# A state scan beside a feed-forward network: the sum over states one step earlier, background operations two or three steps later

## The reference

```python
x = layernorm(x + L0_attn(x))                                   # attention phase of the kernel
x = layernorm(x + (silu(x @ W1.T) * (x @ W3.T)) @ H @ W2.T)     # first network
# state scan, 32 states for each of the 512 features, 4 sequences of 512 tokens
delta = softplus(dt + b_dt)
h = exp(delta_t * A) * h + (delta_t * u_t) * B_t                # one step in t
y_t = einsum('bdn,bn->bd', h, C_t)
x = layernorm(x + y + u * D_param)
x = layernorm(x + (silu(gate) * up) @ w_down.T)                 # second network
```

## Time and profile before

| | us |
|---|---|
| median of 3 runs | 2284.1 |
| lowest and highest | 2273.91 and 2285.38 |
| the profiled execution | 2278.88 |
| its span | 2277.1 |
| TensorE busy in it | 2058.8 |
| VectorE, ScalarE, GpSimd busy | 1482.9, 956.8, 1333.1 |

### The profile page before, as it was taken

One profiled execution on the slowest core, in us unless ns is written; L12 is line 12 of the kernel. 1 busy time (PEld: TensorE's weight loads), 2 busy tenths in 40 slices (PEclk: granted clock), 3 DMA queues, 4 the chain that ended last, 5 costly groups with the idle time before them and its releaser, 6 DMA issues. The chain is left out here.

```text
span 2277.1 us, 27746 instructions
## 1 busy us (share of the span) xinstructions
PE 2058.8 (90%) x9456; PEld 1272.9 (56%) x9456; DVE 1482.9 (65%) x1794; ACT 956.8 (42%) x1597; POOL 1333.1 (59%) x1015
## 2 busy tenths in 40 slices
PE   8899999589998899888989889998899999999997
PEld 6767676357854444444444445444455555456785
DVE  2525325244337878687877889877889999995333
ACT  4333231343245445544556454445445544443212
POOL 4222311245317977688877898656887798683210
PEclk9899999799999999998999999999999999999999
DMA  5000100346634455455545554323434334333552
GB/s 192 20 19 19 37 18 9 130 157 239 247 137 141 170 178 179 144 163 183 157 163 179 188 174 148 110 83 98 148 125 139 107 123 137 120 135 129 184 184 77
DMA packets 100607, 301.20 MB, mean 132 GB/s; under 512 B 25792, under 2 KB 38592, under 8 KB 83712
## 3 DMA queue, kind: packets, MB, share of 16 engines
q1 hardware_dynamic: 100480, 299.62, 38.9%
HBM read 228.28 MB, written 71.30 MB: 132 GB/s over the span
## 5 line engine op out<-in xcount | busy, mean ns | idle before, releaser
L1461 POOL TENSOR_TENSOR h_times_c<-h_states,c_rep 128x512 f32<-128x512 f32 x512 | 667.4, 1319 | 285.5 <-PE scan_y L1100 265.1
L1233 ACT ACTIVATE delta_spread<-delta_spread,a_neg 128x512 f32<-128x512 f32 x512 | 338.7, 662 | 336.8 <-PE delta_spread L1072 335.9
L1345 DVE TENSOR_TENSOR d_b<-du_spread,b_rep 128x512 f32<-128x512 f32 x384 | 263.6, 687 | 90.9 <-PE du_spread L1091 83.9
L1423 POOL TENSOR_TENSOR h_lo<-silu_in_h_lo,h_hi 128x512 fp32r<-128x512 f32 x128 | 171.3, 1338 | 255.1 <-ACT h_hi L1159 255.1
L1315 DVE TENSOR_TENSOR x<-x,y_or_aux 128x512 f32<-128x512 f32 x256 | 171.8, 671 | 182.2 <-PE y_or_aux L80 182.2
L78 PE MATMUL gate<-x_hi,w 128*128 128x512 f32 x512 | 278.2, 543 | 7.4 <-POOL x_lo L1428 5.2
L78 PE MATMUL y_or_aux<-h_hi,w 128*128 128x512 f32 x512 | 263.4, 514 | 21.2 <-ACT b_rep L1201 12.2
L1365 DVE TENSOR_TENSOR_SCAN h_states<-delta_spread,d_b 128x512 f32<-128x512 f32 x192 | 233.6, 1217 | 66.1 <-ACT delta_spread L1233 61.0
L78 PE MATMUL up<-x_hi,w 128*128 128x512 f32 x512 | 270.0, 527 | 0.0
L1365 DVE TENSOR_TENSOR_SCAN h_states<-delta_spread,h_last,d_b 128x512 f32<-128x512 f32 x192 | 244.7, 1277 | 33.3 <-ACT delta_spread L1233 33.1
L1072 PE MATMUL delta_spread<-stack,selectors 96*128 96x512 bf16 x512 | 202.6, 396 | 68.3 <-DVE h_states L1365 67.6
(11 more groups left out here) (158 smaller groups left out, 3710.9 us busy)
## 6 DMA issues: line engine op xcount, KB each, us to landing
w<-w_split SPq DMA_DIRECT2D x112, 1024.0 KB, 4.8
w<-w_split SPq DMA_DIRECT2D x112, 512.0 KB, 5.7
w_split<-w_presplit SPq DMA_DIRECT2D x48, 512.0 KB, 3.9
w_split<-w SPq DMA_DIRECT2D x16, 1024.0 KB, 6.3
spread_parts<-squares_or_parts SPq DMA_DIRECT2D x16, 768.0 KB, 4.0
stack<-spread_parts SPq DMA_DIRECT2D x96, 128.0 KB, 5.3
h_times_c<-in_w13a SPq DMA_DIRECT2D x16, 512.0 KB, 4.3
w_split<-w SPq DMA_DIRECT2D x16, 512.0 KB, 6.5
```

Source lines behind the costliest of these rows:

```text
L1233: act.activation(dl[:, s % ND], dl[:, s % ND], ACT.Exp, scale=a[:, column(s):column(s) + 1]).then_inc(s_da, 1)
L1345: dve.tensor_tensor(db[:, by_dve(s) % NB], uu[:, i % NU], brep[:, tile_of(s // SPO) % 2], ALU.mult).then_inc(s_db, 1)
L1423: pool.tensor_tensor(hl[:, idx % 4], sg[:, idx % 4], hh[:, idx % 4].bitcast(F32), ALU.subtract).then_inc(s_hl, 1)
L1461: pool.tensor_tensor(hc[:, s % NC_], hs[:, s % NH], crep[:, tile_of(s // SPO) % 2], ALU.mult).then_inc(s_hc, 1)
```

## The change

The same instructions in another order. `LAG` goes from 6 to 5, so the sum of quad q stands in scan step 4q + 8. Parts: `part_high` in P + 2 and P + 3, `part_rest` in P + 3 and P + 4, `part_mid` in P + 5 and P + 6, `part_low` in P + 6 and P + 7, the store in P + 8; `step_size` and `step_input` stay at P and P + 1. Presplit weights: high cast T + 4, rest T + 5, store T + 6, and in SyncE's step the store now stands ahead of a load; the load stays at T. Norms of width 1: squares from b + 3 instead of b + 2, variance in b + 9 instead of b + 6, scaling behind it; width 2 is as before. The tables for what follows a norm move by two to six steps. The load of the next stack stands in step 18 of 32 instead of 14.

```diff
@@ -652,17 +652,17 @@
...
-NORM_TICK = (-11, 4, 16, 28, 109, 205, 274, 301, 403, 415, 493, 532, 589, 658, 685, 781)
+NORM_TICK = (-11, 4, 16, 28, 109, 205, 277, 301, 403, 418, 493, 532, 589, 658, 685, 781)
...
-PARTS_TICK = ((121, 139, 147, 155), (236, 244, 252, 260), (332, 340, 348, 356), (445, 452, 459, 466))
...
+PARTS_TICK = ((121, 139, 147, 155), (239, 247, 255, 263), (335, 343, 351, 359), (449, 455, 461, 467))
...
@@ -679,14 +679,15 @@
     return [start + k // width for k in range(KD)]
+SQUARE_DELAY, VAR_DELAY = {1: 3, 2: 1}, {1: 9, 2: 3}
...
-VAR_AT = {b + 3 * (3 - w): e for e, (b, w) in enumerate(zip(NORM_TICK, NORM_WIDE))}
+VAR_AT = {b + VAR_DELAY[w]: e for e, (b, w) in enumerate(zip(NORM_TICK, NORM_WIDE))}
 CENTRE_AT, SQUARE_AT, SCALE_AT = {}, {}, {}
 for e_, (b_, w_) in enumerate(zip(NORM_TICK, NORM_WIDE)):
     for k_ in range(KD):
         CENTRE_AT.setdefault(stretch(b_ + 1, w_)[k_], []).append((e_, k_))
-        SQUARE_AT.setdefault(stretch(b_ + 3 - w_, w_)[k_], []).append((e_, k_))
-        SCALE_AT.setdefault(stretch(b_ + 3 * (3 - w_) + 1, w_)[k_], []).append((e_, k_))
+        SQUARE_AT.setdefault(stretch(b_ + SQUARE_DELAY[w_], w_)[k_], []).append((e_, k_))
+        SCALE_AT.setdefault(stretch(b_ + VAR_DELAY[w_] + 1, w_)[k_], []).append((e_, k_))
...
@@ -696,7 +697,7 @@
 PRE_AT = at_tick(PRE_TICK)
-SCALE_TICK_END = {e: b + 3 * (3 - w) + 1 + (KD - 1) // w for e, (b, w) in enumerate(zip(NORM_TICK, NORM_WIDE))}
+SCALE_TICK_END = {e: b + VAR_DELAY[w] + 1 + (KD - 1) // w for e, (b, w) in enumerate(zip(NORM_TICK, NORM_WIDE))}
 PARTS_BEFORE_NORM = [sum(tick < b for row in PARTS_TICK for tick in row) for b in NORM_TICK]
...
@@ -765,7 +766,7 @@
     w13x = nc.dram_tensor("w13_split", (2, NC, P, 2, 2, KD * P), F32, kind="Internal").ap()
     w2x = nc.dram_tensor("w2_split", (2, NC, P, 2, D), F32, kind="Internal").ap()
     parts_d = nc.dram_tensor("spread_parts", (NO, P, 2, 3, TT), BF16, kind="Internal").ap()
-    ND, NU, NB, NH, NC_, LAG = 2, 2, 2, 6, 7, 6
+    ND, NU, NB, NH, NC_, LAG = 2, 2, 2, 6, 7, 5
     W13, W2 = 3, 4
     with ExitStack() as ctx:
         p = Prog(nc, ctx)
@@ -946,16 +947,16 @@
                         w13_load((tick + 13) // 6)
                     if pos < HC and NC <= HC * unit + pos < CHUNKS:
                         w2_load(HC * unit + pos)
+                    if tick - 6 in PRE_AT:
+                        pre_store(PRE_AT[tick - 6])
                     if tick in PRE_AT:
                         pre_load(PRE_AT[tick])
-                    if tick - 4 in PRE_AT:
-                        pre_store(PRE_AT[tick - 4])
-                    if tick - 6 in PARTS_AT:
-                        parts_store(*PARTS_AT[tick - 6])
-                        if PARTS_AT[tick - 6] in ((0, 0), (0, 1)):
-                            stack_load(PARTS_AT[tick - 6][1])
+                    if tick - 8 in PARTS_AT:
+                        parts_store(*PARTS_AT[tick - 8])
+                        if PARTS_AT[tick - 8] in ((0, 0), (0, 1)):
+                            stack_load(PARTS_AT[tick - 8][1])
                     o, step = divmod(tick - SCAN_TICK, SPO)
-                    if step == 14 and 2 <= o + 1 < NO:
+                    if step == 18 and 2 <= o + 1 < NO:
                         stack_load(o + 1)
                     for e in NORM_AT_END:
                         if tick == SCALE_TICK_END[e]:
@@ -1285,16 +1286,16 @@
                         w2_high((tick - 1) // 6)
                     if tick in SOFT_AT:
                         soft(*SOFT_AT[tick])
-                    if tick - 1 in PARTS_AT:
-                        part_high(*PARTS_AT[tick - 1], 0)
                     if tick - 2 in PARTS_AT:
-                        part_high(*PARTS_AT[tick - 2], 1)
+                        part_high(*PARTS_AT[tick - 2], 0)
                     if tick - 3 in PARTS_AT:
-                        part_mid(*PARTS_AT[tick - 3], 0)
-                    if tick - 4 in PARTS_AT:
-                        part_mid(*PARTS_AT[tick - 4], 1)
-                    if tick - 2 in PRE_AT:
-                        pre_high(PRE_AT[tick - 2])
+                        part_high(*PARTS_AT[tick - 3], 1)
+                    if tick - 5 in PARTS_AT:
+                        part_mid(*PARTS_AT[tick - 5], 0)
+                    if tick - 6 in PARTS_AT:
+                        part_mid(*PARTS_AT[tick - 6], 1)
+                    if tick - 4 in PRE_AT:
+                        pre_high(PRE_AT[tick - 4])
             @block.vector
             def _(dve):
@@ -1482,16 +1483,16 @@
                         w13_low((tick + 10) // 6)
                     if (tick - 2) % 6 == 0 and 0 <= (tick - 2) // 6 < NC:
                         w2_low((tick - 2) // 6)
-                    if tick - 2 in PARTS_AT:
-                        part_rest(*PARTS_AT[tick - 2], 0)
                     if tick - 3 in PARTS_AT:
-                        part_rest(*PARTS_AT[tick - 3], 1)
+                        part_rest(*PARTS_AT[tick - 3], 0)
                     if tick - 4 in PARTS_AT:
-                        part_low(*PARTS_AT[tick - 4], 0)
-                    if tick - 5 in PARTS_AT:
-                        part_low(*PARTS_AT[tick - 5], 1)
-                    if tick - 3 in PRE_AT:
-                        pre_low(PRE_AT[tick - 3])
+                        part_rest(*PARTS_AT[tick - 4], 1)
+                    if tick - 6 in PARTS_AT:
+                        part_low(*PARTS_AT[tick - 6], 0)
+                    if tick - 7 in PARTS_AT:
+                        part_low(*PARTS_AT[tick - 7], 1)
+                    if tick - 5 in PRE_AT:
+                        pre_low(PRE_AT[tick - 5])
```

More of the change, by code:

```diff
@@ L659 @@
 NORM_AT_END = (10, 12, 14, 15)
-SPLIT_TICK = (-6, 11, 166, 270, 366, 474, 544, 664)
-RANK_TICK = (115, 217, 313, 427)
-DT_TICK = ((118, 127, 130, 133), (220, 223, 226, 229), (316, 319, 322, 325), (430, 433, 436, 439))
-STATES_TICK = ((121, 124), (232, 235), (328, 331), (442, 445))
-SOFT_TICK = (((119, (0,)), (135, (1, 2, 3))), ((231, (0, 1, 2, 3)),), ((327, (0, 1, 2, 3)),), ((441, (0, 1, 2, 3)),))
-PARTS_TICK = ((121, 139, 147, 155), (236, 244, 252, 260), (332, 340, 348, 356), (445, 452, 459, 466))
+SPLIT_TICK = (-6, 11, 167, 275, 370, 475, 547, 664)
+RANK_TICK = (115, 220, 316, 433)
+DT_TICK = ((118, 127, 130, 133), (223, 226, 229, 232), (319, 322, 325, 328), (436, 439, 442, 445))
+STATES_TICK = ((121, 124), (235, 238), (331, 334), (448, 451))
+SOFT_TICK = (((119, (0,)), (135, (1, 2, 3))), ((234, (0, 1, 2, 3)),), ((330, (0, 1, 2, 3)),), ((447, (0, 1, 2, 3)),))
+PARTS_TICK = ((121, 139, 147, 155), (239, 247, 255, 263), (335, 343, 351, 359), (449, 455, 461, 467))
 PRE_BLOCKS = 3 * NC
```

## The result

The changed kernel took 2304.9 us (median of 4 runs, 2298.4 to 2308.4) beside 2279.8 for the kernel before in the same comparison: ratio 1.0107, 95% interval 1.0068 to 1.0146. It is slower by 25 us where 52 us of gain were forecast, and lies outside the range. The profiled execution took 2308.4 us, span 2306.6.

What follows compares the result with a forecast made beforehand. Bound: waits among engines in the scan, 127.8 us TensorE idle plus at most 41 us of low clock. Stretch gains of 60 us, less 6 (presplit) and 2 (start), gave 52: 2278.9 to 2227 us, range 2195 to 2250.

Steps and rivals of the forecast that it cites:

- part 4: Presplit weights: SyncE reaches the store later, in about a third of 48 blocks behind a 1 MB load; net cost 6 us.
- parts 1 to 3: Earlier sum, later parts steps and later norms in the scan: shorter waits, together 60 us of gain summed by stretch.
- the third rival: Presplit store lands behind weight loads: 16 blocks, 4 us of ScalarE waiting each, half felt: 32 us, 2253; chance 0.09.
- the fifth stretch: Scan from 1246 to 1371 us, with parts work: loss 24 us, cap 12 by GpSimd's load, forecast gain 9.
- part 5: Start of the scan: first part's casts, lows and store two steps later; cost 2 us, bounds 0 and 3.7.
- The second and third stretch: Scan from 769 to 955 us, store's waits, gain 6; and 955 to 1070 us, parts work, gain 18.
- The last: The rest of the scan, after 1665 us: loss 13 us, mostly norm work that stays; forecast gain 3.
- Part 1: LAG 6 to 5: GpSimd one step, 1.86 us at least, closer to TensorE; most d_b product waits within reach.
- Parts 2 and 3: Parts: waits of 4.47 or 2.3 us shrink under 1 or go; norms: centring waits near 1.3 us should go.
- Part 6: Stack loads four steps later still have eight steps, at least 15 us, before the first spread reading them: cost nothing.
- GpSimd as the bound: First rival: GpSimd, 91% busy from 1246 to 1371 us, stays late; parts stretches give 12 instead of 38: 2253; chance 0.13.
- the second rival: VectorE starved by GpSimd: ten of 16 step sizes 5.1 us longer, +51 against some 26 of gain: 2304; chance 0.10.

Runs made afterwards that it cites:

- e5: The kernel before with only the presplit weights' cast, rest and store two steps later, as in the changed kernel: 2311.6 us, ratio 1.0160.
- e3: The changed kernel with the presplit weights' cast, rest and store, and SyncE's order, put back to the old steps: 2250.6 us, ratio 0.9873.
- e4: e3 with LAG back at 6, so only the parts and norms are as in the changed kernel: 2266.9 us, ratio 0.9941.
- e1: The kernel before with LAG 5 alone: 2283.1 us, ratio 1.0034.
- e10: e3 with `leave` one step earlier, in step 6 of an output block instead of 7: 2247.3 us, ratio 0.9859.
- e12: e10 with squares and variances of the width 1 norms back at their old distances: 2251.2 us, ratio 0.9868.

## Why the prediction was wrong, point by point

**The step that failed is part 4, the presplit weights**: "I take a net cost of 6 us and keep 0 to 32 for the range." It measured 36 us alone (e5, 28 to 45 by the interval) and 53 in the changed kernel (e3), above the upper bound. Of the 77 us between the forecast gain of 52 and the measured loss of 25, 47 are this part; some 28 are parts 1 to 3. The place was named rightly (SyncE stands at the next load and reaches the store behind a weight load) and so was the third rival; its size was wrong in three terms.

The first is the count. The prediction has a load of 1 MB before the store in about a third of the 48 blocks. By the written order that is right, 14 blocks; but it leaves out the 512 KB loads, of which 14 more stand there. Together they are 28 loads, in 22 blocks, two in 6 of them, whatever the engines do. The second is the delay. The prediction gave ScalarE about 4 us in 16 blocks, 64 us; the store landed 3.6 us later behind one load and 4.5 behind two (7.9 and 8.8 us after the rest instead of 4.3), so the price of a block was near right, but there were 22 of them. Most of it is the store's own way, 6.9 and 7.5 us from issue to landing instead of 3.9; its issue comes only 0.5 and 1 us later. The third is the share that reaches TensorE. The prediction took half of ScalarE's waiting; from e3 to the kernel after the wait grew by 60 us (43.1 to 102.8) and the time by 53, nearly all of it, and from the kernel before to e5 the wait grew by 53 and the time by 36, two thirds. The scan's exponentials stand behind the waiting cast, and the clock fell too (0.89 in the fifth stretch; 0.92 at the same steps in e3).

**Parts 1 to 3** were to give 60 us in all and gave some 32: e3 is 29 below the kernel before, with some 3 us for the start (part 5) already paid. By stretches e3 against before reads:

```profile
776.50:949.40 172.90, 163.82 (x705) 87.42 (x704) 147.56 (x174) 90.38 (x178) 149.63 (x118) 0.99 0.55 185
949.40:1046.20 96.80, 84.93 (x357) 45.08 (x356) 83.74 (x93) 53.83 (x100) 85.96 (x69) 0.93 0.55 188
...
1218.40:1348.20 129.80, 109.95 (x453) 58.68 (x452) 109.84 (x118) 66.30 (x108) 111.46 (x89) 0.92 0.53 179
...
1536.10:1633.00 96.90, 87.16 (x367) 46.38 (x366) 80.48 (x96) 55.48 (x103) 85.00 (x68) 0.95 0.40 139
1633.00:2040.60 407.60, 383.55 (x1703) 210.37 (x1702) 371.83 (x431) 184.36 (x314) 312.08 (x244) 1.00 0.36 122
```

The same steps took 186, 117, 125, 104 and 396 us before. The second and third stretch gave 13 and 20, more than the 6 and 18 forecast; the seventh 7 of 11. The fifth was to give 9 and lost 5: VectorE is busy 8 us longer there with the same instructions (101.8 to 109.8), while GpSimd, named as the cap, is 86% busy (91% before). The last, outside the presplit and the parts, was to give 3 and lost 12, and that goes with LAG: at the same steps it takes 396 and 399 us with LAG 6 (e5, e4) and 405 and 408 with LAG 5 (e1, e3), and TensorE stands idle for 24 us there in e3 instead of 12. GpSimd's waits for VectorE's scan in this stretch rise from 2.8 us in one wait to 33.6 in 38. No run shows why the closer order loses here what it gains elsewhere.

**Part 1** had two errors. "I cost this wait at nothing" held for the products: no wait of TensorE for them is among its larger ones, and the shortest gap from product to sum is 3.5 us where 2.2 were forecast. But the sum has a second condition that I did not price: the first sum of a block overwrites the PSUM bank that `leave` reads, and `leave` did not move. That is the new wait of 15.4 us in 8; its removal in e10 brought 3 us. The larger error is in what a GpSimd close behind VectorE does to VectorE. The prediction reasoned that such a GpSimd "runs out of ready work sooner". It does (its waits for VectorE's scan go from 19.8 us in 9 to 125.4 in 100 in e1), and yet it lengthens VectorE's two-operand instructions more (53 to 82 us of stretching in e1).

**Parts 2 and 3** held in mechanism: the wait for the rest of the parts went from 32.3 to 3.7 us, that for centring from 48.1 to 19.8. Together they gave 13 us (e4); the norms' share is 2 to 4 (e12), which can't be told from none.

**Part 5** forecast 2 us with bounds 0 and 3.7. From the first rank matmul to the first decay spread 40.4 us passed before, 43.9 in e4, 44.0 in e3 and 45.8 after. But it is 42.4 in e1 and 42.2 in e5, which keep the parts' old distances; so these cost between 1.6 and 3.6, and the forecast may well be right. It showed ahead of the store, not behind it (store to first spread 9.4 us, 9.7 before), so the sign that I gave for it pointed at the wrong place. **Part 6** held: TensorE's only wait for a stack load is the one at the start, 2.7 us (1.2 before).

**The rivals.** The third held, at nearly twice its price (26 us above the forecast's 6, measured 47 above). The second gave 2304 us, and the kernel took 2304.9, by coincidence: its mechanism is worth some 64 us in e10, which is 32 us faster than the kernel before, and most of the stretching (53 of 78 us) was there before the change. GpSimd as the bound is not shown: in the fifth stretch, where a gain stayed out, it is 86% busy in e3.

**The signs that were named** for part 4 told the truth: a wait of 100 us and more was to mean the third rival, and it is 102.8. GpSimd's wait for the sum did turn into waits for VectorE's scan (106.7). The d_b product's wait was to fall under a third and fell to under a half; the third stretch was to fall under 15 us of idle time and has 18.9 (104.5 less 85.6). The step sizes gave a mixed sign: their median stayed at 1.35 us, under 2, but the longest took 7.72, over the 6.5 that was to speak for the second rival. The sign for being wrong, idle time that stays, came true in the scan (140.1 us), though with other waits in front.

What stays open: how much of the 53 us is the lower clock and how much the waits themselves. The lower level lasted 148 us in e3 and 205 in the kernel after, so it can hold 28 us at most; no run holds the clock fixed. Nor was it tried to give the store a queue of its own.

## What to carry to other kernels

When a step is moved later on an engine that issues DMAs in order, look at what it is moved behind, not only at how far: every transfer that stands between in the written order goes first, and the one you moved lands behind all of them. Count all of them, small ones too, from the order before you run; here that count, 28, could be read from the step tables. Putting the store back behind its load was worth 47 us here, and moving the whole chain, load included, cost nothing that could be measured. And an order that brings GpSimd closer behind VectorE has to be weighed against VectorE's instructions with two operands from SBUF: the same edit, LAG 5, cost 8 us or gave 16 or 21, depending on what stood beside it.

## What the runs showed of the hardware that was not expected

A VectorE instruction with two operands from SBUF does not get in between GpSimd instructions that follow one another without a gap: a 128x512 one of 0.69 us took 7.72 us while six of GpSimd's, 1.3 us each, went through. The same engine reducing one operand of the same size took 659 to 686 ns in all 16 cases, 14 of them beside a GpSimd instruction; the same operation with one of its two operands in PSUM took 658 to 693 ns in all 384 cases, 318 of them beside a GpSimd instruction. The Trainium skill says in "SBUF — State Buffer", section "Who interferes with whom", that a VectorE instruction with two inputs from SBUF contends with a GpSimd instruction that reads SBUF, and that the order of issue decides which of the two is blocked; the trace agrees, and shows besides that VectorE's can stay blocked over several GpSimd instructions in a row.

The 512 KB store's way from issue to landing took 3.9 us in the median of the 26 stores that had no weight load issued between, 6.9 behind one load of 512 or 1024 KB (16 stores) and 7.5 behind two (6 stores). In e3 the same 22 stores, without loads between, took 4.1 and 5.0.
